# Base counts and turned cells behind the first group of block products, and one fp32 product a source block for the moments of p

## The reference

```
ef = concat([x[row], x[col], edge_attr])          # 200000 x 258
h = ef @ W1 + b1
mu, var = mean(h, axis=0), mean((h - mu) ** 2, axis=0)
h = relu((h - mu) * rsqrt(var + eps) * gamma + beta)
msgs = h @ W2 + b2
out0 = segment_sum(msgs, row) / (counts + 1) + x
x = layernorm(x + out0)
deg = in-degree + 1;  norm = rsqrt(deg)[src] * rsqrt(deg)[dst]
conv(h, W, b) = segment_sum((h @ W)[src] * norm, dst) + b
x = layernorm(x + conv(relu(conv(relu(conv(x, W0, b0)), W1, b1)), W2, b2))
```

## Time and profile before

| | |
|---|---|
| median of 3 runs | 3799.39 us (3799.33 to 3801.58) |
| the profiled execution's own time | 3800.09 us |
| its span, first to last instruction | 3798.3 us |
| TensorE busy | 3624.6 us (95%) |
| VectorE busy | 2510.9 us (66%) |
| ScalarE busy | 1500.2 us (39%) |
| mean granted clock of TensorE | 0.987 |

### The profile page before, as it was taken

How to read it: one execution, slowest core, us unless ns; L and a number is a source line. 1 busy time by engine, 2 the same in 40 slices (tenths; PEclk the granted TensorE clock), 3 DMA queues, 4 the chain that set the end, 5 groups by cost and what they waited for, 6 DMA issues and landing times.

```text
span 3798.3 us, 104239 instructions
## 1 busy us (share of the span) xinstructions
PE 3624.6 (95%) x40722; PEld 2585.7 (68%) x40943; DVE 2510.9 (66%) x3683; ACT 1500.2 (39%) x3822; POOL 962.0 (25%) x916
## 2 busy tenths in 40 slices
PE   4699999999998899999999999999999999999999
PEld 4588888888888677777777777774444544454444
DVE  6999999999995798898889888973111111111112
ACT  5355555455554466666666666662000000000000
POOL 3000000000000566676767667710000000000000
PEclk8899999999999899999999999999999999999999
DMA  7122322332234455555555555535666566656664
GB/s 246 53 88 87 101 87 85 97 91 87 85 103 148 136 156 157 157 155 156 158 156 154 159 157 156 153 134 182 197 195 200 187 199 196 200 183 211 205 208 133
DMA packets 428707, 569.35 MB, mean 150 GB/s; under 512 B 193778, under 2 KB 353452, under 8 KB 421708
## 3 DMA queue, kind: packets, MB, share of 16 engines
q1 hardware_dynamic: 396908, 510.29, 43.2%
q0 software_dynamic: 25088, 51.43, 5.0%
q10 hardware_dynamic: 6624, 6.42, 0.5%
HBM read 458.48 MB, written 109.53 MB: 150 GB/s over the span
## 4 chain that ended last, share of the span: by engine, by line
PE 92%; DVE 4%; ACT 1%; issue 1%; SPq 1%; DMA 1%; POOL 0%; ACTq 0%; DVEq 0%; POOLq 0%
PE py L1674 31%; PE ph L1364 11%; PE pY L861 11%; PE pSum L1383 10%; PE pbk L922 8%; PE ph L1367 7%; PE pA L848 3%; PE ph L1359 3%; PE pX L853 2%; PE pS L852 1%; PE pbk L899 1%; PE pbk L898 1%; ACT x L1030 1%; DVE prod_raw L1152 1%; PE pg L1660 1%
## 5 line engine op out<-in xcount | busy, mean ns | idle before, releaser
L1312 POOL DMA_INDIRECT q<-pq_dram,chosen x784 | 846.6, 1080 | 385.4 <-issue 198.5
L1674 PE MATMUL py<-ring_raw,p 128*128 128x512 bf16 (+1 forms) x3822 | 785.5, 368 | 4.7 <-DVE g L1792 2.8
L1364 PE MATMUL ph<-p,prod_raw 128*128 (+1 forms) x7056 | 683.2, 219 | 18.6 <-DVE prod_raw L1480 11.9
L1674 PEld LDWEIGHTS py<-ring_raw,p 128*128 128x128 bf16 x3822 | 362.6, 98 | 419.2 <-issue 4.4
L1364 PEld LDWEIGHTS ph<-p,prod_raw 128*128 128x128 bf16 x7056 | 492.6, 98 | 117.3 <-issue 0.7
L1428 ACT ACTIVATE x<-ph 128x512 bf16<-128x512 f32 x588 | 351.4, 598 | 454.2 <-PE ph L1367 320.7
L1367 PE MATMUL ph<-q,prod_raw 128*128 128x128 bf16 x4704 | 519.4, 219 | 0.0
L861 PE MATMUL pY<-p,ring_raw 128*128 128x128 bf16 x7203 | 501.7, 219 | 0.8 <-POOL ring_raw L793 0.4
L1383 PE MATMUL pSum<-x,ring_raw 128*128 128x384 bf16 x2401 | 498.8, 327 | 0.3 <-DVE x L1537 0.3
L1532 DVE SCALAR_TENSOR_TENSOR ring_raw<-ph,x 128x512 f32<-128x512 f32 x588 | 404.2, 687 | 121.2 <-ACT x L1428 121.2
L1850 DVE TENSOR_TENSOR yt<-py,dinv_row 128x512 f32<-128x512 f32 (+1 forms) x39 | 25.8, 661 | 684.1 <-PE py L1674 684.1
(11 more groups left out here) (338 smaller groups left out, 4407.9 us busy)
## 6 DMA issues: line engine op xcount, KB each, us to landing
ring_raw<-at_dram SPq DMA_DIRECT2D x252, 896.0 KB, 4.8
at_dram<-ring_raw SPq DMA_DIRECT2D x49, 1568.0 KB, 5.6
prod_raw<-lrow_dram SPq DMA_DIRECT2D x147, 384.0 KB
prod_raw<-lrow_dram SPq DMA_DIRECT2D x196, 256.0 KB
prod_raw<-lrow_dram SPq DMA_DIRECT2D x49, 416.0 KB
q<-pq_dram,chosen POOLq DMA_INDIRECT x784
arow_dram<-x SPq DMA_DIRECT2D x294, 36.8 KB
x<-arow_dram SPq DMA_DIRECT2D x147, 54.0 KB
```

What stands on the lines that cost most here:

```text
L1312: nc.gpsimd.indirect_dma_start(q_rows[i][:, k, :], None, pq_rows, bass.IndirectOffsetOnAxis(ap=chosen[u][:, i, k:k + 1], axis=0)).then_inc ...
L1364: last = nc.tensor.matmul(bank[:, k * P:(k + 1) * P], T[q][:, 0, at:at + P], p_b[:, :, m3, :].rearrange("p a d -> p (a d)"), start=False, ...
L1674: last = nc.tensor.matmul(py[par][:, 0:w], g3[c % 2][:, 7 * i + m, k, :], ring[i][:, 0:w // P, m, :], start=at == m == k == 0, stop=at == ...
```

## The change

It has two parts that do not touch each other.

1. In a step of the first pass the base counts and the transposes of the cells are taken out of `step` into `bases`, which `both` calls after group 0 (its block products and its y products) on TensorE. ScalarE's copies of the bases and of the turned cells follow its evacuation of group 0. In steps without block products (s < 2) they stay ahead of everything, but for the two small projections.

2. For the moments of p, ScalarE no longer squares p but scales each block of it by the nodes' edge counts (the scale is a column of `mom`), and puts `mom` itself beside it: 131 columns. TensorE makes one fp32 product a block, with p stationary (128 columns). Its result holds the three weighted sums of p in its last 3 columns, one feature to a partition, and on its diagonal the count-weighted sum of the squares. VectorE copies the 3 columns (`p_sums`), a small product turns them, and VectorE masks the diagonal with the identity (`own`), which a product with ones sums up.

```diff
@@ TensorE, pe_1
-                    def both(s, par, half, a_, y_):
-                        ...
-                    def step(s, m, par, bkt, h_, a_, y_, st_):
-                        moments(s, par, y_, st_)
+                    def bases(s, m, par, bkt, h_):
                         if bkt:
                             pe.wait_ge(S["hot_ready"], s + 1)
                             if not (isinstance(s, int) and s == 0):
                                 pe.wait_ge(S["cells_ready"], s)
...
+                    def both(s, m, par, half, bkt, h_, a_, y_):
+                        if a_:
+                            pe.wait_ge(S["hsd_ready"], (s - 2) * 2 + (half + 1))
+                            if half == 0 and not (isinstance(s, int) and s < 3):
+                                pe.wait_ge(S["t_read"], s - 2)
+                        groups = neighbours(s, par, half) if a_ else range(*HALVES[half])
+                        for g in groups:
+                            if y_:
+                                if g == 0:
+                                    pe.wait_ge(S["a_final"], s - 2)
+                                    if not (isinstance(s, int) and s < 4):
+                                        pe.wait_ge(S["y_kept"], s - 3)
+                                y_group(s, par, g)
+                            if g == 0:
+                                bases(s, m, par, bkt, h_)
...
-                        both(s, par, 0, a_, y_)
-                        both(s, par, 1, a_, y_)
+                        both(s, m, par, 0, bkt, h_, a_, y_)
+                        both(s, m, par, 1, bkt, h_, a_, y_)
@@ ScalarE, act_1
+                    def bases(s, m, par, bkt, h_):
+                        if bkt:
+                            act.wait_ge(S["base_ready"], s + 1)
+                            nc.scalar.activation(base_2[:].rearrange("p h k u -> p (h k) u"), pbk[:, BASE:BASE + 2 * B].unsqueeze(2).to_broadcast([P, 2 * B, 2]), ACT.Copy).then_inc(S["based"], 1)
+                        if h_:
+                            act.wait_ge(S["turned"], s)
+                            if not (isinstance(s, int) and s < 3):
+                                act.wait_ge(rows_out[1 - par], 128 * (m - (1 - par)))
+                            nc.scalar.activation(rows_t[1 - par][0:2 * BW, :, :].rearrange("p j s -> p (j s)"), ptr[0:2 * BW, 0:4 * P], ACT.Copy).then_inc(S["rows_ready"], 1)
...
                             nc.scalar.activation(abuf[u][:, 4 * g:4 * g + w, :], pA[(g + u) % 2][:, 0:w * P].rearrange("p (b d) -> p b d", d=P), ACT.Copy).then_inc(S["a_ready"], 1)
+                            if g == 0:
+                                bases(s, m, par, bkt, h_)
...
                         if a_:
-                            evacuate(s, m, par)
+                            evacuate(s, m, par, bkt, h_)
+                        else:
+                            bases(s, m, par, bkt, h_)
@@ buffers of the stretch between the passes
-                psq = [x1_free[:, u * 7 * D:(u + 1) * 7 * D].rearrange("p (j d) -> p j d", d=D) for u in range(2)]
+                psq = [x1_free[:, u * 7 * (D + 3):(u + 1) * 7 * (D + 3)].rearrange("p (j d) -> p j d", d=D + 3) for u in range(2)]
...
+                own, p_sums = bt[0][:], bt[1][:, 0:3]
@@ TensorE, pe_2
                         for j in range(7):
-                            nc.tensor.matmul(pSum[0][0:3, 0:D], mom[:, 7 * i + j, :], pf[:, 7 * i + j, :], start=i == j == 0, stop=i == j == 6)
-                            last = nc.tensor.matmul(pSum[1][0:3, 0:D], mom[:, 7 * i + j, :], psq[i % 2][:, j, :], start=i == j == 0, stop=i == j == 6)
+                            last = nc.tensor.matmul(pSum[0][:, 0:D + 3], pf[:, 7 * i + j, :], psq[i % 2][:, j, :], start=i == j == 0, stop=i == j == 6)
                         last.then_inc(S["square_used"], 1)
...
                     pe.wait_ge(S["weighed"], 2)
+                    nc.tensor.matmul(pSum[1][0:3, 0:D], p_sums, ident_f[:], start=True, stop=True).then_inc(S["p_turned"], 1)
+                    pe.wait_ge(S["weighed"], 3)
+                    nc.tensor.matmul(st[:, D:2 * D], ones_f[:], own, start=False, stop=False)
+                    pe.wait_ge(S["weighed"], 4)
                     nc.tensor.matmul(st[:, 0:D], ones_f[0:3, :], xs[0:3, 2 * D:3 * D], start=False, stop=False)
-                    nc.tensor.matmul(st[:, D:2 * D], ones_f[0:3, :], xs[0:3, 0:D], start=False, stop=False)
-                    nc.tensor.matmul(st[:, D:2 * D], ones_f[0:3, :], xs[0:3, D:2 * D], start=False, stop=True).then_inc(S["stats_made"], 1)
+                    nc.tensor.matmul(st[:, D:2 * D], ones_f[0:3, :], xs[0:3, 0:D], start=False, stop=True).then_inc(S["stats_made"], 1)
@@ ScalarE, act_2
+                    act.wait_ge(S["moments_in"], 1)
                     for i in range(7):
                         if i >= 2:
                             act.wait_ge(S["square_used"], i - 1)
-                        nc.scalar.activation(psq[i % 2][:], pf[:, 7 * i:7 * i + 7, :], ACT.Square).then_inc(S["squared"], 1)
+                        for j in range(7):
+                            nc.scalar.activation(psq[i % 2][:, j, 0:D], pf[:, 7 * i + j, :], ACT.Copy, scale=mom[:, 7 * i + j, 0:1])
+                        nc.scalar.activation(psq[i % 2][:, :, D:D + 3], mom[:, 7 * i:7 * i + 7, :], ACT.Copy).then_inc(S["squared"], 1)
@@ VectorE, dve_2
                     dve.wait_ge(S["square_used"], 7)
-                    for u in range(2):
-                        link(V.tensor_tensor(xs[0:3, u * D:(u + 1) * D], cf[0:3, u * D:(u + 1) * D], pSum[u][0:3, 0:D], ALU.mult))
-                    link(V.tensor_tensor(xs[0:3, 2 * D:3 * D], cf[0:3, D:2 * D], pSum[0][0:3, 0:D], ALU.mult))
+                    V.tensor_copy(p_sums, pSum[0][:, D:D + 3]).then_inc(S["weighed"], 1)
+                    V.tensor_tensor(own, pSum[0][:, 0:D], ident_f[:], ALU.mult).then_inc(S["weighed"], 1)
+                    dve.wait_ge(S["p_turned"], 1)
+                    link(V.tensor_tensor(xs[0:3, 0:D], cf[0:3, 0:D], pSum[1][0:3, 0:D], ALU.mult))
+                    link(V.tensor_tensor(xs[0:3, 2 * D:3 * D], cf[0:3, D:2 * D], pSum[1][0:3, 0:D], ALU.mult))
                     V.memset(dummy2[:], 0.0).then_inc(S["weighed"], 1)
```

More of the change, by code:

```diff
@@ L575, in build @@
         fit_sem = lambda n: fit_stack.enter_context(nc.semaphore(n))
-        S.update({n: fit_sem(n) for n in """phase2 rows_set quad_summed dv2 moments_in squared square_used weighed stats_made bn_sqrt bn_rooted bound_ready credits t_ready hf_ready
+        S.update({n: fit_sem(n) for n in """phase2 p_turned rows_set quad_summed dv2 moments_in squared square_used weighed stats_made bn_sqrt bn_rooted bound_ready credits t_ready hf_ready
              mm_done z_hi z_res z_mid z_low sum_done sum_taken credits3 node_done dinv_made dinv_turned dinv_kept dinv_out dinv_in s_turned s_copied s_made cg_taken c_squared x1_made ga_made g_hi g_res g_mid x_rest0 x_rest1
@@ L908, in step, with moments @@
                             last.then_inc(S["turned"], 1)
+                    def both(s, m, par, half, bkt, h_, a_, y_):
[13 more added lines that the diff above has]
+                                bases(s, m, par, bkt, h_)
+                    def moments(s, par, y_, st_):
+                        if st_:
+                            pe.wait_ge(S["y_kept"], s - 3)
+                            last = nc.tensor.matmul(pM[:, 0:2 * D + 7], qp[par], ym[par], start=False, stop=False)
+                        if isinstance(s, int) and s == B + 3:
+                            last = nc.tensor.matmul(pM[:], onesb[:], zerob[:, 0:2 * D].unsqueeze(1).to_broadcast([P, 2, 2 * D]), start=False, stop=True)
+                        if st_:
+                            last.then_inc(S["m_used"], 1)
+                    def step(s, m, par, bkt, h_, a_, y_, st_):
+                        moments(s, par, y_, st_)
                         if isinstance(s, int) and s == 1:
@@ L973, in act_1, with evacuate @@
                             nc.scalar.activation(q3st[(g - 1) % 4][:, 0:w, 1, :], rq[u][:, 0:w, :], ACT.Copy).then_inc(S["mid"], 1)
-                    def evacuate(s, m, par):
+                    def bases(s, m, par, bkt, h_):
[7 more added lines that the diff above has]
+                            nc.scalar.activation(rows_t[1 - par][0:2 * BW, :, :].rearrange("p j s -> p (j s)"), ptr[0:2 * BW, 0:4 * P], ACT.Copy).then_inc(S["rows_ready"], 1)
+                    def evacuate(s, m, par, bkt, h_):
                         c, u = s - 2, par
@@ L994, in step @@
                             last.then_inc(S["known_ready"], 1)
[L995 to L1000, removed]
-                            nc.scalar.activation(rows_t[1 - par][0:2 * BW, :, :].rearrange("p j s -> p (j s)"), ptr[0:2 * BW, 0:4 * P], ACT.Copy).then_inc(S["rows_ready"], 1)
                         if isinstance(s, int) and s == 1:
```

## The result

The changed kernel took 3785.86 us (median of 6 runs) against 3800.14 of the kernel before (6 runs): a ratio of 0.9961, 95% interval 0.9948 to 0.9975. One of the six took 16238.05 us, for a reason that no trace shows, and is left out of the ratio and the interval. The forecast was 3786.7. The profiled execution took 3785.86 us with a span of 3784.0, 14.3 less than before.

A forecast was written before the change was run, and what follows sets the result against it. TensorE was taken as the bound (92% of the chain), VectorE 0.2 us a step behind. Gains of 8.0 + 4.7 = 12.7 off 3800.1 give 3787.4, less 0.7 is 3786.7; own range 3783 to 3790, outer 3781 to 3794.

The forecast's parts named there:

- Hole and hiding work: First pass: TensorE's 0.56 us a step of waiting for copied cells is filled by moved work; its own step becomes 21.64.
- rival C: First pass: VectorE is no bound and the whole hole is returned, 25 us, and 4.7: 3770; chance 0.04.
- VectorE next: First pass: VectorE, 0.2 us a step behind TensorE, becomes late; period 22.04 to 22.10, gain taken as 6.2 us.
- Rival B: First pass: VectorE's step by itself already is the present period, only the second edit pays, 4.7: 3794.7; chance 0.12.
- The lag: End of first pass: TensorE's last products follow VectorE's ranks by 0.7 us instead of 2.56, a single gain of 1.9.
- ScalarE's new order: First pass: ScalarE's copies of bases and turned cells move behind the first evacuation; claimed to cost nothing.
- the covers: First pass: time between emptying a bank and TensorE wanting it, 0.9 us for group 2 and 0.7 for group 3.
- rival D: First pass: slower, group 0's bank isn't emptied in time behind the filler copies; 2 us late gives 3818; chance 0.04.
- Moments: Moments of p, between the passes: ScalarE bounds at 2.15 us a set; products end at 1254.5 against 1259.95, 5.45 gained.
- Tail: From the last moments product to the last `st` product: 2.8 us against 2.05 today, a cost of 0.75.
- The two rules: Moments of p: skill-page warnings that small idles make the clock oscillate and weight loads cost 10.5 us; either returns nothing.
- rival A: Moments of p: products get no shorter, end 1259.8, a loss of 0.6 there, gain 7.4 in all, 3792; chance 0.08.

The follow-up runs named there:

- e3: Changed kernel with VectorE's product of hot_p and field 6 left out in the 42 looped steps: 3762.18 us, ratio 0.9904 to the kernel before.
- e4: Kernel before with VectorE's product of hot_p and field 6 left out in the 42 looped steps: 3799.05 us, ratio 1.000.
- e5: Changed kernel with the four transposes of the cells made twice on TensorE: 3785.47 us, ratio 0.9968 to the kernel before.
- e6: Kernel before with the four transposes of the cells made twice on TensorE: 3809.05 us, ratio 1.0027.
- e8: Changed kernel with base counts and turned cells behind group 2 instead of group 0, on TensorE and ScalarE: 3804.86 us, ratio 1.0018 to the kernel before.
- e12: Changed kernel with base counts and turned cells behind group 1 and a third psq buffer in its own memory: ratio 0.9971 to the kernel before.
- e1: Kernel before with the first edit alone (bases and turned cells behind group 0), old moments of p: 3791.61 us, ratio 0.9981.
- e2: Kernel before with the second edit alone (one fp32 product a block for the moments of p), old step order: 3794.28 us, ratio 0.9990.
- e9: Changed kernel with base counts and turned cells behind group 1 instead of group 0, on TensorE and ScalarE: ratio 0.9969 to the kernel before.
- e10: Changed kernel with one of VectorE's eight products a step (field 3) made by GpSimd: ratio 1.0194 to the kernel before.
- e11: Changed kernel with field 3's product made by GpSimd and a third psq buffer in its own memory: ratio 1.0186 to the kernel before.

## Why the prediction was right

**Hole and hiding work.** Right: the wait for the cells went to 0.7 us, the group of block products took its place. Its size was under-read, because the list's 0.56 leaves out the 0.16 that lie under the end of a record. TensorE's own step is 21.50, not the 21.64 that 22.20 - 0.56 gave, as e3 shows. Had VectorE not been in the way, rival C would have been worth 0.70 us a step, a quarter more than it was priced at.

**VectorE next.** The step on which the whole forecast hung. 8.5 us of waits in the earlier trace rows said how far VectorE stood behind; forecast 22.04 to 22.10, measured 22.04. e3 to e6 show that it is VectorE, and e3 that nothing else holds the step above 21.50. Rival B (period unchanged) and C (all of it back) fall with the same number.

**The lag.** In the last step the ranks' one-hot is ready at 1164.04 + 2.42 = 1166.46 and TensorE begins line 926 at 1167.04: 0.6, forecast 0.7, before 2.56. The first pass gave 8.7, forecast 8.0: the lag's 2.0 and, over the steps, 6.7 instead of my 6.2. The 0.16 us a step was right; the steps that it pays in are the 42 looped ones and not 45 (42 x 0.16 = 6.7), and the 6.2 had leant towards the one slower step of the earlier trace rows. The other 0.33 of the 9.05 lies ahead of the first step.

**ScalarE's new order.** Cost nothing, as forecast; the covers, forecast 0.9 and 0.7, are 1.28 for group 2 and 0.85 for group 3. TensorE wants both banks when I said (2.84 and 3.94 us after hot_p, forecast 2.8 and 3.9). It is the evacuations that end sooner, at 1.56 and 3.09 instead of 1.9 and 3.2, and this is a slip in the prediction's sum: cells copied at -0.9 and 2.0 us of filler copies make +1.1, not +1.4. It made rival D look nearer than it was and changed nothing else. e8 shows that they are needed and what it costs when one is gone.

**Moments.** Forecast 5.45, measured 5.3: last product 18.6 us after the first copy, forecast 18.5. ScalarE's sets came at 2.16, forecast 2.15. TensorE's set shows as 1.84 us, where I had 1.6, but that is a set behind a wait. Two sets of e12 without one between them, at full clock, start 1.58 apart:

```profile
1235.11 1.74 PE L1338 MATMUL pSum<-psq,prod_raw 128*128 128x131 f32 x14
1236.69 3.08 PE L1338 MATMUL pSum<-x,prod_raw 128*128 128x131 f32 x23
```

So the 1.6 was right, and so were the 0.55 us to spare a set: 2.16 - 1.58 = 0.58, of which the list shows 0.31 to 0.32.

**Tail.** Forecast 0.75, measured 0.8.

**Luck.** The two edits gave 8.7 + 5.3 - 0.8 = 13.2 us, forecast 12.7. The other 1.1 of the 14.3 was in no term of the sum: 0.33 is scatter from one execution to another that happened to fall the same way, and the 0.76 is unexplained. The 5.3 depends on the execution too: the old moments took 24.0 us in the kernel before and 25.4 in e1, as the clock rose early or late, and the new ones 18.6 in both the changed kernel and e2. The prediction took the 24.0 of one trace for fixed.

**The two rules.** Frequent small idles did not make the clock oscillate: it stayed at 1.00 through five of them, and rival A's 1259.8 did not come. The Trainium skill's section on it ("TensorE: Matmul & The Clock Gate", A second HAM failure mode: psum-queue depth-cycling) tells of bf16 products of 512 columns in another kernel; for these fp32 products and idle times of 0.31 to 0.49 us a set the trace shows nothing of the kind. Nor did the wide weight loads come into the open: a set of seven products took 1.84 us. By that page of the Trainium skill (LDWEIGHTS) seven times the estimated 0.21 on top of 1.6 would be 3.1.

**What stays open.** Whether the 0.76 us between the two stretches is the new order's or scatter, what made e9 to e12 longer, and what held up the one run of 16238.05 us.

## What to carry to other kernels

When a wait of the bounding engine is filled, the gain is capped by the engine that comes next, and the trace of before tells the cap: add up the waits of every other engine for this one (here 0.2 us a step on VectorE against a hole of 0.7, which the list showed as 0.56), and count the lag between the two once more, at the end. Work put into a hole may also be the cover of something else: before moving it on by another place, lay out which bank, buffer or queue gets its time from standing behind it, as two groups further on turned a gain of 14 us into a loss of 6. Judge a change of bound from both sides, by taking work from the new bound and giving some to the old one, in the kernel before as well as after.

## What the runs showed of the hardware

- The idle time that the list shows for TensorE is less than what the stall costs: 0.37 recorded against 0.54 (e3), 0.56 against 0.70 in the kernel before, 0.74 against 0.90 in e8. The difference is the 0.16 us by which a record of 0.83 us outlasts the start of the next one (0.67 us later) where TensorE does not wait.
- Idle times of TensorE of 0.31 to 0.49 us between sets left the clock at 1.00 in the changed kernel. In e12 the clock was still 1.00 when the products began again after 2.10 us of idle, and at 0.50 about 0.9 us later; it stayed there through the next idle time of 2.76 us.
- Seven fp32 products with 128 stationary and 131 moving columns took 1.58 us at a granted clock of 1.00 when nothing stood between two sets (e12), and 1.84 from the first record's start to the last one's end behind a wait.
- A GpSimd multiplication of 128x1666 bf16 elements took 3.73 us beside VectorE and stretched VectorE's three of the same size from 2.89 to 5.67. GpSimd was busy for only 28.96 us of the 542.00 between 621 and 1163 us of the changed kernel, and yet its idle time was of no use for this work.
